# Weight magnitudes in the first turn of each batch, weights rounded before the second block starts, and its first batch ahead of the norm's rest

## The reference

```
x = x + L1_xattn(ln(x), ctx, mask)     # scores clipped to +-50, softmax, output projection,
                                       # then a layer norm of the projected delta (gamma, beta)
x = x + L1_ffn(ln(x)):
  weight_quant(w): s = 1 / mean(|w|);            wq = clip(round(w * s), -1, 1) / s
  act_quant(x):    s = 127 / max(|x|, last axis); xq = round(x * s) / s
  h = relu(act_quant(x) @ weight_quant(w1).T)    # 512 -> 2048
  out = act_quant(h) @ weight_quant(w2).T        # 2048 -> 512
```

## Time and profile before

| | us |
|---|---|
| median of 3 runs | 2395.26 (2393.09 to 2398.01) |
| the profiled execution's own time | 2396.35 |
| span of the profiled execution | 2394.5 |
| layer 1's attention, batches 0 to 7 (first exponentials to last output) | 826.6 to 1068.7 |
| attention's tail | 1068.7 to 1106.8 |
| feed-forward block up to its last residual | 1106.8 to 1202.5 |

### The profile page before, as it was taken

The page is one execution under the profiler, slowest core; times in us unless marked ns, Lnnn a source line. Parts: engine busy times, 40 slices in busy tenths (PEclk is TensorE's granted clock), DMA queues, the critical chain, the costliest instruction groups (busy, mean ns, idle before and its releaser), DMA issues.

```text
span 2394.5 us, 39229 instructions
## 1 busy us (share of the span) xinstructions
PE 2101.5 (88%) x14719; PEld 1693.1 (71%) x14719; DVE 1086.1 (45%) x2401; ACT 911.3 (38%) x1738; POOL 495.7 (21%) x358
## 2 busy tenths in 40 slices
PE   6989999896996888987978999889987999979997
PEld 5976666686445777775566777789986999945554
DVE  4447667565114255558825666422332555511111
ACT  3346556433222344455645454332233322222221
POOL 2233232232231211100031110033322111013322
PEclk7889999998997899978989999899999999989998
DMA  3110010127224121122020000021121100379995
GB/s 107 58 39 26 13 38 1 54 66 278 74 84 129 43 88 45 49 86 111 20 65 23 26 25 2 27 75 57 45 75 43 35 25 13 110 244 311 324 317 152
DMA packets 90860, 203.68 MB, mean 85 GB/s; under 512 B 9198, under 2 KB 14418, under 8 KB 88594
## 3 DMA queue, kind: packets, MB, share of 16 engines
q1 hardware_dynamic: 80562, 174.82, 22.4%
q0 software_dynamic: 10144, 26.75, 4.2%
HBM read 183.84 MB, written 19.53 MB: 85 GB/s over the span
## 4 chain that ended last, share of the span: by engine, by line
PE 65%; DMA 11%; DVE 10%; ACT 7%; issue 5%; POOL 1%; SPq 1%; ACTq 0%; DVEq 0%; POOLq 0%
PE psum L106 15%; PE psum L107 13%; PE psum L109 13%; DMA l3f_sum_dram<-l3f_y,l3f_rows 8%; PE psum L887 3%; PE psum L3376 2%; PE psum L2608 2%; PE psum L3346 2%; PE psum L2068 1%; PE psum L913 1%; PE psum L2273 1%; PE psum L1528 1%; DVE l2x_highest L2150 1%; PE psum L3362 1%; DVE ln_stats L145 1%
## 5 line engine op out<-in xcount | busy, mean ns | idle before, releaser
L1528 PE MATMUL psum<-l3f_gate_up,l3f_x_turned 128*128 128x352 f32 x496 | 154.2, 464 | 0.8 <-ACT l3f_x_turned L1587 0.8
L1528 PEld LDWEIGHTS psum<-l3f_gate_up,l3f_x_turned 128*128 128x128 f32 x496 | 93.0, 193 | 48.1 <-issue 1.7
L3135 POOL TENSOR_TENSOR l0x_w_lo<-l0x_w_raw,l0x_w_hi 128x512 fp32r<-128x512 f32 x52 | 71.8, 1398 | 152.0 <-ACT l0x_w_hi L3388 127.5
L2109 ACT ACTIVATE l2x_probs<-psum,l2x_shift 100x361 f32<-100x361 f32 x128 | 65.0, 559 | 98.2 <-DVE l2x_shift L2154 97.0
L3490 ACT ACTIVATE l0x_probs<-l0x_probs,l0x_lowest 100x361 f32<-100x361 f32 x128 | 75.1, 588 | 59.8 <-DVE l0x_lowest L3654 59.6
L106 PE MATMUL psum<-xn_hi,l2f_w_gu_hi 128*128 128x400 f32 x256 | 89.7, 350 | 8.8 <-ACT l2f_silu L588 4.9
L1802 POOL TENSOR_TENSOR l2x_ctx_lo<-l2x_ctx_raw,l2x_ctx_hi 128x1448 fp32r<-128x1448 f32 x8 | 26.3, 3289 | 339.8 <-ACT l2x_ctx_hi L1810 339.7
L107 PE MATMUL psum<-xn_lo,l2f_w_gu_hi 128*128 128x400 f32 x256 | 88.8, 347 | 0.0
L1503 POOL DMA_INDIRECT l3f_sum_dram<-l3f_y,l3f_rows x31 | 49.2, 1587 | 183.3 <-DMA l3f_sum_dram<-l3f_y,l3f_rows 143.6
L1554 PE MATMUL psum<-l3f_down,l3f_h_turned 128*128 128x512 f32 x186 | 85.1, 593 | 0.9 <-DVE l3f_h_turned L1619 0.9
L443 POOL TENSOR_TENSOR l2f_w_gu_lo<-l2f_raw_gu,l2f_w_gu_hi 128x512 fp32r<-128x512 f32 x32 | 43.0, 1353 | 203.6 <-ACT l2f_w_gu_hi L458 203.6
(11 more groups left out here) (533 smaller groups left out, 6181.1 us busy)
## 6 DMA issues: line engine op xcount, KB each, us to landing
l3f_gate_up<-in_slabs_dram SPq DMA_DIRECT2D x31, 1280.0 KB, 7.8
l3f_down<-in_slabs_dram SPq DMA_DIRECT2D x31, 512.0 KB
l0x_w_raw<-in_slabs_dram SPq DMA_DIRECT2D x52, 256.0 KB, 2.8
l0f_weights<-in_slabs_dram SPq DMA_DIRECT2D x8, 1536.0 KB
l1x_piece<-in_bit_w_dram SPq DMA_DIRECT2D x8, 1024.0 KB, 4.8
l1f_raw<-in_bit_w_dram SPq DMA_DIRECT2D x8, 1024.0 KB, 9.0
l2f_raw_gu<-in_slabs_dram SPq DMA_DIRECT2D x32, 256.0 KB, 2.6
l3f_down<-in_slabs_dram SPq DMA_DIRECT2D x31, 192.0 KB
```

The source lines that it names most:

```text
L1528: mm = pe.matmul(c.psum[:, bank + x, 0:self.INNER], self.x_turned[:, t % 2, k, :], self.gate_up[:, q, at:at + self.INNER], start=k == 0, s ...
L2109: act.activation(self.probs[:, m % 2, g, :], c.psum[0:S, g, 0:C], ACT.Exp, bias=self.shift[:, g:g + 1], scale=self.SCALE).then_inc(self.s( ...
L3135: pool.tensor_tensor(self.w_lo[:, place, :], self.w_raw[:, n % 3, :], self.w_hi[:, place, :], ALU.subtract).then_inc(self.s("w_split"), 1)
```

## The change

Five things move; no arithmetic is added.

- Magnitudes: slab b is summed in turn 0 of batch b instead of turn 3. Slab 6 comes in turn 2 of batch 5 and slab 7 in turn 0 of batch 6, so batch 7 has none. SP issues the first piece ahead of the output weights' slabs 14 and 15.
- Mean: the sum stands in DVE's turn 0 of batch 7, PE's total in turn 1, DVE's scale in turn 2, and ACT scales slab 0 in turn 3.
- Slabs: SP fetches slabs 0 to 3 as soon as the attention's keys, values and all scores but batch 7's are made, and 4 to 7 once its last output is rounded. All eight are scaled and rounded in the attention's tail.
- Norm: the tail also makes rows 0 and 1 of the feed-forward block's norm. Its PSUM banks become 4, 5, 6 for all batches.
- Feed-forward start: batch 0 is quantised and multiplied when rows 0 and 1 are there; PE turns batches 5 to 7 behind batch 0's first product, and ACT makes rows 4 to 7 behind its relu.

```diff
 sync body (Attention.sync)
+            self.sync_batch(c, sp, b)
             if isinstance(b, int) and b == 0:
                 for i in (14, 15): ...
-            self.sync_batch(c, sp, b)
 BoundedAttention
+    def pieces_in(self, b):
+        return {5: [5, 6], 6: [7], 7: []}[b] if isinstance(b, int) and b > 4 else [b]
+    def nearly_over(self, c, sp):
+        sp.wait_ge(self.s("ctx_split"), B)
+        sp.wait_ge(self.s("k_units"), B * KD)
+        sp.wait_ge(self.s("v_units"), B * 3)
+        sp.wait_ge(self.s("s_units"), (B - 1) * KD)
 act_batch
-            if m == 3:
-                self.act_magnitude(c, act, b)
+            if m % 2 == 0:
+                for j in self.pieces_in(b)[m // 2:m // 2 + 1]:
+                    self.act_magnitude(c, act, j)
+            if m == 3 and not more:
+                act.wait_ge(c.sem("sets_cleared"), self.index)
+                act.wait_ge(self.s("round"), 1)
+                c.apart(act)
+                self.bits.act_scaled(c, act, 0)
 act_finish
-        (shift x4) root_table; act_scaled 0..3; half_rows(0); act_scaled 4, 5; half_rows(1); act_scaled 6
+        act_scaled 1..3; root_table; act_scaled 4..6; half_rows(0); (shift x4); act_scaled 7; half_rows(1)
+        then.deviation(act, 0)
+        then.normalise(act, 0)
+        then.normalise(act, 1)
 dve_finish
-        dve_sum; read(0, 0); dve_step; read(0, 1); whole 0; read(0, 2); whole 1; read(0, 3); read(1, 0)
+        whole 0, 1; read(0, 0); read(0, 1); whole 2; read(0, 2); whole 3; read(0, 3); whole 4; read(1, 0)
...
+        then.moments(dve, 0)
+        self.bits.dve_whole(c, dve, 7)
+        then.inverse(dve, 0)
         apply(1)
 BitFfn.prefetch
         for j in range(2 * KD):
+            if j == KD:
+                sp.wait_ge(c.sem("l1x_o_lo"), B * KD)
 BitFfn.pe
-        for b in range(3, 7): turn; (row 0 made) turn(7)
+        for b in (3, 4):
+            pe.wait_ge(c.sem("ln_rows"), self.norm.before + b - 2)
+            self.norm.turn(pe, b)
...
+                if first_batch:
+                    for b in range(5, B):
+                        pe.wait_ge(c.sem("ln_rows"), self.norm.before + b - 2)
+                        self.norm.turn(pe, b)
 BitFfn.dve body
-            if isinstance(i, int) and i == 0:
-                for j in range(5, 2 * KD):
-                    self.dve_whole(c, dve, j)
```

More of the change, by code:

```diff
@@ L2262, in pe_batch @@
                 self.pe_values(pe, b + 1, 1 - q, m)
+            if m == 1 and not more:
+                pe.wait_ge(c.sem("sets_cleared"), self.index)
+                c.apart(pe)
+                self.bits.pe_total(c, pe)
             pe.wait_ge(self.s("exps"), i * 3 + 3)
@@ L2353, in dve_batch @@
                 low(m - 1, i - 1)
+            if m == 0 and not more:
+                dve.wait_ge(c.sem("sets_cleared"), self.index)
+                dve.wait_ge(self.s("magnitudes"), B)
+                c.apart(dve)
+                self.bits.dve_sum(c, dve)
+            if m == 2 and not more:
+                self.bits.dve_step(c, dve)
             at = m % 2 * 200
@@ L2394, in pe_finish @@
         n, then = self.after, c.norms[self.index + 1]
[L2395 to L2399, removed]
+        for m in range(KD):
             self.pe_out_unit(c, pe, 0, m)
@@ L2451, in apply @@
                                          ALU.mult, ALU.add).then_inc(self.s("applied"), 1)
[L2452 to L2455, removed]
+        for j in range(2):
+            self.bits.dve_whole(c, dve, j)
         read(0, 0)
-        self.bits.dve_step(c, dve)
         read(0, 1)
-        self.bits.dve_whole(c, dve, 0)
+        self.bits.dve_whole(c, dve, 2)
         read(0, 2)
-        self.bits.dve_whole(c, dve, 1)
+        self.bits.dve_whole(c, dve, 3)
         read(0, 3)
+        self.bits.dve_whole(c, dve, 4)
         read(1, 0)
@@ L2831, in body @@
                 for n, k in [(n, k) for n in range(self.CHUNKS) for k in range(KD)]:
-                    if first_batch and k == 0:
-                        pe.wait_ge(c.sem("ln_rows"), self.norm.before + n + 4)
-                    elif k == 0:
+                    if not first_batch and k == 0:
                         pe.wait_ge(self.s("inner"), (i - 1) * self.CHUNKS + n + 1)
@@ L2877, in first @@
         def first():
[L2878 to L2881, removed]
             turned(0)
[L2883 to L2886, removed]
+            self.norm.deviation(act, 1)
+            self.norm.normalise(act, 2)
+            self.norm.normalise(act, 3)
         def body(i, before, now, after):
@@ L2896, in body @@
                                    scale=self.one(self.x_step, i)).then_inc(self.s("inner"), 1)
+                if isinstance(i, int) and i == 0:
+                    half_rows(self.norm, act, 1)
                 act.wait_ge(self.s("h_scales"), i * 3 + 3)
@@ L2937, in whole_x @@
         def whole_x(b):
-            dve.wait_ge(c.sem("ln_rows"), self.norm.before + (b + 1 if isinstance(b, int) and b == 0 else B))
+            dve.wait_ge(c.sem("ln_rows"), self.norm.before + (b + 1 if isinstance(b, int) and b < 2 else B))
             dve.tensor_reduce(self.one(self.x_max, b), row(b), AX.X, ALU.max,
@@ L2950, in body @@
         def body(i, before, now, after):
-            if after:
+            if after and not (isinstance(i, int) and i == 0):
                 whole_x(i + 1)
@@ L2983, in first @@
             dve.tensor_copy(self.identity[:, :], c.identity[:, :]).then_inc(self.s("identity"), 1)
-            n.moments(dve, 0)
-            for g in (1, 2):
-                n.stats(dve, 2 * g)
-                n.stats(dve, 2 * g + 1)
-                n.inverse(dve, g - 1)
-                n.moments(dve, g)
+            whole_x(0)
+            n.stats(dve, 2)
+            n.stats(dve, 3)
+            n.moments(dve, 1)
+            n.stats(dve, 4)
+            n.inverse(dve, 1)
+            whole_x(1)
+            n.stats(dve, 5)
+            n.moments(dve, 2)
             n.inverse(dve, 2)
-            whole_x(0)
             n.stats(dve, 6)
```

35 lines of the change are left out of this document (16 added, 19 removed).

## The result

| | us |
|---|---|
| before, median of 5 runs beside it | 2395.26 (2393.09 to 2398.01) |
| after, median of 5 runs | 2372.35 (2365.85 to 2377.68) |
| ratio, 95% interval | 0.9901 (0.988 to 0.9921) |
| span of the profiled execution | 2370.5 (own time 2372.35) |
| after, all 15 runs on three occasions | 2372.8 |

The forecast was 2375.5 with a range of 2370.0 to 2384.5: faster, and of the right size.

What follows compares the result with a forecast made beforehand. PE, busy for 88% of the span, bounds the kernel, with magnitude sums making it wait between batches. Gains of 11.7 + 8.0 + 0.4 = 20.1 us from 2395.26 give 2375.2, stated as 2375.5, range 2370 to 2384.5.

Steps and rivals of the forecast that it cites:

- Six sums out of the chain: Ends of attention batches 0, 1, 3, 4, 5, 6: magnitude sums leave the chain, gaining 11.7 us.
- The clock: Five stretches behind waits between batches: products mostly at 1.2 GHz regain full clock, gaining 8.0 us, bounds 0 and 9.2.
- Rival 1: Batch borders: waits shrink to 0.6 us but products behind stay half-speed; gain 12.1, 2383.2 us; chance 0.18 in full.
- The sum at nothing in the first turn: ACT in first turns: the 1.99 us sum fits into 2.53 us of idle time, 0.5 left, costing nothing.
- Rival 2: First turns: ACT's sum ends last there too, delaying `xn_hi`; 6.3 us slower in full, 2401.5; chance 0.05.
- Mean in batch 7: Batch 7's turns: DVE's added reduction costs 0.3 us, PE's total leaving the projection gains 0.3; they cancel.
- Tail: Attention's tail: a fifth rounding and the norm's rows 0 and 1 on DVE make the residual ready 1.1 us later.
- Start: Feed-forward start: first product 4.8 us earlier, DVE's maxima 1.8 later; with the tail worth 0.4, bounds -1.6 to 5.4.
- Rival 3: Feed-forward start: batch 0's products get full speed, nearly all 4.8 us reaches the second batch; 2370.5 us; chance 0.10.
- Rival 4: Feed-forward start: the norm's longer chain reaches the third batch, 3 us less gain; 2378.5, inside the forecast's 0.62.
- rival 5: Batch borders: sums stay in the chain at some, bounded by a few tenths per border; no chance of its own.
- Sum: Whole kernel: total predicted gain of 20.1 us, 11.7 + 8.0 + 0.4.

Runs made afterwards that it cites:

- sums-alone kernel: The kernel before with only the magnitude sums moved into first turns, tail and feed-forward start as before; 2377.61 us, and 2371.26 us when run again.
- doubled kernel: The changed kernel with each magnitude sum done twice in its new place in the first turn; 2387.14 us, ratio 0.9976.
- norm first: The changed kernel, but the norm's rest is finished before batch 0 is quantised at layer 1's feed-forward start; 2370.45 us, ratio 0.9909.

## Why the prediction held, step by step

- *Six sums out of the chain, 11.7 us:* right. The five waits shrank by 1.89, 1.90, 1.89, 1.88 and 1.89, together 9.45 us. At the sixth border, which has no values product, the sums-alone kernel's two traces are 1.9 and 1.8 us shorter than the one of before, which makes 11.2 to 11.3. The waits are 0.56 (forecast 0.6) to 1.35 (1.3).
- *The clock, 8.0 with bounds 0 and 9.2:* the mechanism was right, and the size for this execution was the upper bound, as batch 0's border also kept its clock. It did in seven of the nine executions with the sums moved, and fell in two, so half of 2.3 was somewhat low. That this one execution reached the upper bound is chance. The prediction takes a wait of 0.61 us ahead of other products for the nearest row; the trace of before had nearer ones, the same products in batch 0's first two turns at 829.67 and 837.58, behind waits of 0.83 and 0.44 us and both at a clock of 1.00. Rival 1 is refuted for short waits: 35 border waits of 0.81 us or less over all kernels kept the clock, and all 11 of 2.39 us or more lost it. It has a true core between them: of 31 waits from 1.17 to 1.96 us ahead of values products ten kept it and 21 fell, with no order by length (one of 1.83 kept it, one of 1.17 lost it). The Trainium skill (TensorE: Matmul & The Clock Gate, section What's actually happening) says that the windows in which the activity is watched run freely, and that the moment of the change therefore depends on where in a window the first product falls. These rows agree in so far as equal waits of 1.35 and of 1.42 us ended both ways. What decides between them stays open.
- *The sum at nothing in the first turn, 0.5 us left:* right, 0.45 to 0.78 measured, and doubling it showed both that the margin is real and what lies behind it. Rival 2 did not happen, but the doubled kernel realised its mechanism.
- *Mean in batch 7, +0.3 - 0.3:* mis-sized. PE's total now runs at half clock in batch 7's second turn. The way from the first turn's weighted sum to the second's is 4.51 us with it and 4.01 and 4.14 in the two traces of the sums-alone kernel, so it costs 0.4 to 0.5 us, and the tail, which it left, got no shorter.
- *Tail, +1.1:* from the first output product to the residual it is 0.6 in the first pair (38.3 against 37.7), and 1.0 to 1.3 against the 37.3 and 37.0 of the sums-alone kernel.
- *Start:* measured with the tail's 0.6 included, as the forecast did, PE's first product came 4.9 us earlier (forecast 4.8) and stayed slow at 6.40 us; DVE's maxima 1.75 later (1.8), PE's second product 1.5 later (1.8), the second batch's last maximum 0.2 earlier (0.4). Rival 3, batch 0 really running ahead, is refuted: its product ran at a granted clock of 0.56. The upper bound of this part was added up wrongly: the second product's 5.58 us leave 2.0 over 3.6, not 2.5, so 4.9 and not 5.4. Rival 4, the start as a loss, did not show in the second column, and of rival 5 nothing is left, since no sum stands in the chain. Tail and start together were put at 0.4. Five traces with the new order average 131.9 us in the second column, five with the old 132.1. Behind that small sum stand two larger terms that I had not priced apart. From the residual to the second batch's last maximum it is 30.6 us before, 27.2 with the norm first and 29.8 in the changed kernel. The 3.4 us between the first two go with the three roundings' leaving DVE, though about 1 us of them is the shorter first product (5.19 us instead of 6.16), and no run moves the roundings alone; the order of batch 0 and the norm's rest takes 2.6 back.
- *Sum, 20.1:* the first trace has 20.3 from the second values product to the end of the feed-forward block, the two later ones 19.0 and 18.5; the one lost the clock at batch 0's border (4.60 instead of 3.07 us), the other behind the jump back (4.72 instead of 3.08). The medians say 21 to 23. The 2 us between fall into columns that the change doesn't touch and that scatter by more; which of it is real is open.

## What to carry to other kernels

Filler work belongs where its engine is idle and the engine behind it does not wait: read the idle time in brackets ahead of the next instruction, and place there only what is shorter. Here 1.9 us of filler in the wrong turn cost 3.4 us each, because PE's wait was followed by slow products, and taking half of the filler out of the wrong place won back about a fifth of the time (4.6 of 21 to 23 us), not half. When work is moved ahead on one engine, look at what the next engine has queued ahead of its own part; interleaving DVE's maxima was worth 2.8 and 4.3 us of that stretch in two executions, and running PE ahead alone cost 2.6 in one.

## What the runs showed of the hardware

- The granted clock behind a wait of PE is not a function of the wait's length between 1.17 and 1.96 us, and no transfer beside it is needed for it to fall (0.63 at a DMA share of 0.00) nor does one make it fall (1.00 at 0.83).
- The same binary differs between executions in such places: 3.07 and 4.60 us for the same stretch, behind the same 1.35 us.
- PE's stall at the loop's jump back was between 4.32 and 4.79 us in all thirteen executions, whatever stood around it. The way from the last values product ahead of it to the next border's, without that border's wait, lay between 45.2 and 48.1 us in the twelve executions with no doubled sum in it, longest where the first products behind the jump ran at a clock of 0.61 to 0.66.
- An accumulating activation over 128x2048 takes 1.90 us and its read of the accumulator 0.19.
